# Global queries of a sparse attention: probabilities turned by transposes in two halves, their output on four column groups

## The reference, cut to what matters

```python
rel = k_idx[None, :] - q_idx[:, None]
local_ok = (rel <= 0) & (rel >= -(lw - 1))            # lw = 128
key_global = (k_idx % gs == 0)[None, :]               # gs = 64
query_is_global = (q_idx % gs == 0)[:, None]
allowed = (local_ok | key_global | query_is_global) & (rel <= 0)
scores = jnp.where(allowed[None, None], scores, -1e9)
w = jax.nn.softmax(scores, axis=-1)
out = jnp.einsum('bhtk,bhkd->bhtd', w, v)
```

## Time and profile before

| what | us |
|---|---|
| median of 3 runs | 3175.98 (3173.67 to 3176.52) |
| the profiled execution | 3170.18 |
| its span, from first to last record | 3168.2 |
| sparse attention in it, first matmul to last copy to `o_sb` | 1932.3 to 2534.9 |

### The profile page before, as it was taken

One profiled execution on the slowest core, in us unless ns is written; L12 is line 12 of the kernel. 1 busy time (PEld: TensorE's weight loads), 2 busy tenths in 40 slices (PEclk: granted clock), 3 DMA queues, 4 the chain that ended last, 5 costly groups with the idle time before them and its releaser, 6 DMA issues. The chain is left out here.

```text
span 3168.2 us, 105574 instructions
## 1 busy us (share of the span) xinstructions
PE 2955.8 (93%) x41356; PEld 2157.6 (68%) x41388; DVE 2607.4 (82%) x5505; ACT 1687.3 (53%) x3301; POOL 1076.7 (34%) x1434
## 2 busy tenths in 40 slices
PE   7989999999999799999997993999999969999999
PEld 4545777777777377777774552777777747777776
DVE  5759999999999499999985994777777669999997
ACT  4654888778887433333333661665665623333333
POOL 3551211212211122222223662555555612222222
PEclk9998999999999899999998996999999979999999
DMA  6664444444443222222223666455555322222221
GB/s 205 219 204 88 94 103 101 102 99 94 94 103 74 73 85 87 83 88 86 84 68 107 202 199 157 119 138 138 139 140 139 99 84 88 83 88 86 83 88 51
DMA packets 362150, 353.35 MB, mean 112 GB/s; under 512 B 79066, under 2 KB 298714, under 8 KB 361642
## 3 DMA queue, kind: packets, MB, share of 16 engines
q1 hardware_dynamic: 356003, 345.15, 39.6%
q10 hardware_dynamic: 5767, 2.68, 0.4%
HBM read 210.85 MB, written 135.27 MB: 109 GB/s over the span
## 5 line engine op out<-in xcount | busy, mean ns | idle before, releaser
L891 DVE TENSOR_REDUCE aA_nmax<-bank 128x1 f32<-128x512 f32 (+3 forms) x1216 | 715.0, 655 | 62.9 <-PE bank L952 56.8
L934 ACT ACTIVATE aA_prob<-bank 128x512 f32<-128x512 f32 (+1 forms) x1216 | 616.3, 581 | 196.2 <-PE bank L952 191.4
L952 PE MATMUL bank<-aA_ks,aA_qs 96*32 96x512 bf16 (+15 forms) x6144 | 512.5, 320 | 16.6 <-DMA aA_ks<-parts_A 12.7
L952 PE MATMUL bank<-aA_qs,aA_ks 99*32 99x512 bf16 (+11 forms) x6144 | 471.4, 314 | 7.0 <-ACT aA_prob L934 3.6
L875 POOL TENSOR_SCALAR_AFFINE_SELECT aA_prob<-aA_prob 128x512 f32<-128x512 f32 x256 | 160.9, 634 | 662.7 <-ACT aA_prob L934 662.7
L952 PE MATMUL bank<-aA_prob,aA_vq 128*32 128x512 f32 (+3 forms) x3072 | 356.1, 489 | 0.9 <-POOL aA_prob L875 0.9
L952 PEld LDWEIGHTS bank<-aA_ks,aA_qs 96*32 96x32 bf16 x6144 | 246.4, 96 | 125.6 <-DVE aA_nmax L891 45.2
L1382 ACT ACTIVATE aB_prob<-bank 128x512 f32<-128x512 f32 (+1 forms) x512 | 262.2, 574 | 88.1 <-PE bank L1421 84.4
L952 PEld LDWEIGHTS bank<-aA_qs,aA_ks 99*32 99x32 bf16 x6144 | 225.3, 96 | 62.6 <-ACT aA_prob L934 20.3
L1288 DVE TENSOR_REDUCE aB_nnear<-bank 128x3 f32<-128x480 f32 (+1 forms) x352 | 208.1, 636 | 57.0 <-PE bank L1421 52.1
L952 PE MATMUL bank<-mask_sb,ident_b 128*32 128x128 bf16 (+3 forms) x4096 | 237.8, 203 | 0.6 <-issue 0.5
(11 more groups left out here) (235 smaller groups left out, 6597.7 us busy)
## 6 DMA issues: line engine op xcount, KB each, us to landing
parts_A<-pA_part SPq DMA_DIRECT2D x96, 256.0 KB, 4.6
aA_qs<-parts_A SPq DMA_DIRECT2D x192, 128.0 KB, 4.0
parts_B<-pB_part SPq DMA_DIRECT2D x96, 256.0 KB, 2.6
aB_qs<-parts_B SPq DMA_DIRECT2D x192, 128.0 KB, 3.2
aA_ks<-parts_A SPq DMA_DIRECT2D x186, 128.0 KB, 4.0
aB_ks<-parts_B SPq DMA_DIRECT2D x186, 128.0 KB, 3.3
o_A<-aA_o_sb SPq DMA_DIRECT2D x32, 512.0 KB, 3.0
o_B<-aB_o_sb SPq DMA_DIRECT2D x32, 512.0 KB, 2.9
```

What stands on the lines that cost most here:

```text
L891: nc.vector.tensor_reduce(dst, src, AX.X, ALU.max, negate=True).then_inc(s["m_taken"], 1)
L934: nc.scalar.activation(dst, src, ACT.Exp, scale=SCALE).then_inc(s["e_taken"], 1)
L952: return nc.tensor.matmul(out, lhsT, rhs, start=start, stop=True, skip_group_check=True)
```

## The change

`gturn` becomes two units of four `nc.tensor.transpose` each (128 x 128, the whole identity as the moving side), one for each half of `pg`, each with its own bank of line "e" and its own copy. The copies read every second column of the bank. `og` becomes 32 narrow matmuls, for each block k of 128 keys and each head one with that head's 32 columns of `vq` as the weights and up to 16 columns of `pgT` as the moving side; the output of head h lies on partitions 32h to 32h + 31, in columns 0 to 15, and one copy takes all. In the table of tasks `gturn` has cost 500 twice (1150 before), ACT's part 400 twice (620), due -0.6 (-0.55); `og` has cost 1000 (1150), DVE's part 170 (500), due -0.4 (-0.35).

```diff
@@ sparse_tasks
         for c in range(2):
-            unit("e", "gexp", c, 180, "act", 710, -0.7, ("dve", "gmax", n, 1), then=[("act", "gturn", pre, 0)])
-        unit("e", "gturn", 0, 1150, "act", 620, -0.55, ("act", "gexp", n, 1), then=[("pe", "og", pre, 0)])
-        unit("m", "og", 0, 1150, "dve", 500, -0.35, ("act", "gturn", n, 0), ("pool", "vq", n, 0),
+            unit("e", "gexp", c, 180, "act", 710, -0.7, ("dve", "gmax", n, 1), then=[("act", "gturn", pre, c)])
+        for c in range(2):
+            unit("e", "gturn", c, 500, "act", 400, -0.6, ("act", "gexp", n, c), then=[("pe", "og", pre, 0)])
+        unit("m", "og", 0, 1000, "dve", 170, -0.4, ("act", "gturn", n, 1), ("pool", "vq", n, 0),
              then=[("dve", "lay", n - 2, 0)])
@@ take_og (DVE)
-                    src = bank_of("m", "og", n, 0)[:, 0:HQ * NGLOB].rearrange("p (h i) -> p h i", h=HQ)
-                    for h in range(HQ):
-                        mine = slice(2 * DH * h, 2 * DH * (h + 1))
-                        ins = nc.vector.tensor_copy(og[n % 2][mine, :], src[mine, h, :])
-                    ins.then_inc(s["m_taken"], 1)
+                    nc.vector.tensor_copy(og[n % 2][:, :], bank_of("m", "og", n, 0)[:, 0:NGLOB]).then_inc(s["m_taken"], 1)
@@ global_copy (ACT)
-                def global_copy(n, _):
-                    act.wait_ge(s["e_made"], after("e", "gturn", n, 0))
+                def global_copy(n, c):
+
+                    act.wait_ge(s["e_made"], after("e", "gturn", n, c))
                     if n >= 1:
                         act.wait_ge(s["m_made"], after("m", "og", n - 1, 0))
-                    nc.scalar.activation(pgT[:, :, :, :].rearrange("p k h i -> p (k h i)"), bank_of("e", "gturn", n, 0),
-                                         ACT.Copy).then_inc(s["e_taken"], 1)
+                    nc.scalar.activation(pgT[:, 4 * c:4 * c + 4, :, :].rearrange("p k h i -> p (k h i)"),
+                                         bank_of("e", "gturn", n, c)[:, ::2], ACT.Copy).then_inc(s["e_taken"], 1)
@@ global_turn, global_out (PE)
-                def global_turn(n, _):
-                    pe.wait_ge(s["e_taken"], max(after("e", "gexp", n, 1), bank_clear("e", "gturn", n, 0)))
-                    out = bank_of("e", "gturn", n, 0).rearrange("p (k i) -> p k i", k=QT)
-                    for k in range(QT):
-                        ins = mul(out[:, k, :], pg[:, k * P:(k + 1) * P], ident[:, ::2], True)
+                def global_turn(n, c):
+                    pe.wait_ge(s["e_taken"], max(after("e", "gexp", n, c), bank_clear("e", "gturn", n, c)))
+                    out = bank_of("e", "gturn", n, c).rearrange("p (k i) -> p k i", k=4)
+                    for k in range(4):
+                        ins = nc.tensor.transpose(out[:, k, :], pg[:, (4 * c + k) * P:(4 * c + k + 1) * P], ident[:, :])
                     ins.then_inc(s["e_made"], 1)
                 def global_out(n, _):
                     pe.wait_ge(s["vq_made"], n + 1)
-                    pe.wait_ge(s["e_taken"], after("e", "gturn", n, 0))
+                    pe.wait_ge(s["e_taken"], after("e", "gturn", n, 1))
                     need(pe, s["m_taken"], bank_clear("m", "og", n, 0))
-                    out = bank_of("m", "og", n, 0)[:, 0:HQ * NGLOB].rearrange("p (h i) -> p h i", h=HQ)
+                    out = bank_of("m", "og", n, 0)
                     for k in range(QT):
 
                         i0 = k * NGLOB // QT
-                        ins = mul(out[:, :, i0:], vq[n % 2][:, k, :, :].rearrange("p h d -> p (h d)"),
-                                  pgT[:, k, :, i0:], k == 0)
+                        for h in range(HQ):
+                            ins = mul(out[32 * h:32 * h + 32, i0:NGLOB], vq[n % 2][:, k, h, :], pgT[:, k, h, i0:], k == 0)
                     ins.then_inc(s["m_made"], 1)
```

## The result

The changed kernel takes 3197.86 us (median of 4 runs, 3196.51 to 3198.37), the kernel before 3174.82 in the same session: a ratio of 1.0073 (95% interval 1.0055 to 1.0090). It is slower by 23 us, where 50 us less had been forecast.

The account below looks back on a forecast made before the run. PE was taken to set the pace in sparse attention; savings of 0.50 (turn) and 1.35 us (output) per group, less 0.25 for waits, gave 32 x 1.60 = 51 us, a median of 3125 us, range 3101 to 3157.

Parts of the forecast that it names:

- What bounds the kernel: Sparse attention: PE sets the pace, with records for 484 of 500 us; DVE and ACT wait for it.
- The turn: Transposes of `pg` on PE: one pass each, 0.85 us per half, saving 0.50 us per group.
- The output on PE: `og` as 64 narrow passes at 11 ns: 0.70 us instead of 2.05, saving 1.35 us per group.
- The rival of a floor of 25 ns per pass: Narrow output passes cost 25 ns each, so the block takes 1.6 us; 3150 in all; chance 0.20.
- I take off 0.25 us per group for that: Sum: allowance for DVE and ACT bursts stopping PE more often, cutting 1.85 us saved per group to 1.60.
- POOL and SP get no work, and no DMA is added or moved: Other engines: the change adds no work for POOL or SP and no DMA, so nothing was counted.
- The slower rival: Halves of the turn stop PE, at 1.25 us each losing 0.65 us per group; 3197; chance 0.07.

Follow-up runs that it names:

- the control without loads: The kernel before, without the loads of q and k after the fourth group: 3170.82 us, ratio 0.9991 to the kernel before.

## Why the prediction was wrong

- **What bounds the kernel**: half right. PE sets the pace of the stage, but it has two limits, its work and its supply of instructions. Before, the supply was sufficient, with little to spare: the control without loads gains nothing and there are only 7 long stops, but packets were used up in as little as 3.1 us, where the next is usable after some 4.1.
- **The turn**: right. One pass per transpose, 0.77 us for a half (0.85 forecast).
- **The output on PE**: right, 0.79 us in the block shown and 0.54 to 0.67 in 17 of 32 groups (0.70). The rival of a floor of 25 ns per pass is refuted: 0.78 / 62 = 12.6 ns in the block shown, 9 to 11 in those 17 groups, with neighbouring passes in different column groups. The Trainium skill, TensorEngine Tiling, section Performance Considerations (Instruction Overhead), gives about 60 cycles per matmul, as an estimate 25 ns at 2.4 GHz; this trace doesn't agree.
- **"I take off 0.25 us per group for that"** is the step that failed. The new "issue" waits were 2.7 us per group, eleven times as much, and neither for line "e" nor for DVE. I had 42.1 us of "issue" in the earlier trace rows, called it a wait with no record that explains it, and didn't ask what it was. The count of records per packet was there to be read before, and so were the 7 long stops.
- **"POOL and SP get no work, and no DMA is added or moved"**: true of data, but 80 more PE instructions per group are DMA traffic too. I had counted passes, at 64 for 16, only as PE time. What I sold as a saving at both blocks, 4 us of 18 in which PE used few instructions, was what kept the supply ahead: no packet was used up in under 3.0 us then, and 26 in about 2.2 us now.
- **The slower rival** gave 3197 and the kernel took 3197.86, but by luck, for a reason that isn't so. It set the stops at the halves of the turn. The waits for the copy to `pgT` there are 4.9 us in 500, halves back to back don't help the narrow output, and the turn alone is faster.
- **The clock** was in no part of the forecast. It fell behind long stops and added some 0.6 us per group, by the estimate above.

## What to carry to other kernels

Count PE instructions, not only PE time, and look at the densest stretch, not at the mean: a packet of 252 must last until the next is there, here about 4 us. Splitting 8 wide matmuls into 32 narrow ones for 1.3 us of work paid in no run with its loads; without them the whole change paid 25 us, but what the split alone pays there wasn't run. "Issue" waits in mid-unit, a packet's worth of records apart, are the sign to look for, and here the loads of data made them worse. Where both limits are close, take the savings that also take instructions away, as the transposes did (16 fewer per group, and with a fitting order 24 us).

## What the runs showed of the hardware

- Instructions reach PE in packets of 16 KB, about 252 matmul and load records each. A packet is under way for 0.96 us; the 40 long stops of the changed kernel end 2.2 to 2.6 us after one has started.
- The next packet starts in the median 1.8 us after PE has begun on the one before, so PE stands where 252 records take less than some 4.1 us (an estimate from the medians). Packets of 2.2 us were followed by a long stop 25 times in 26.
- The same 80 instructions cost 14 us where slow blocks lie between, and 55 us where none do.
- With the DMA share at 0.17 instead of 0.53 the next packet starts 0.5 us sooner, and neither its transfer nor the time from its start to the end of the stop gets shorter (1.01 and 2.45 us, against 0.96 and 2.35). Whether it is bytes, descriptors or their bursts that hold the start up wasn't tried.
- Narrow f32 passes with 2 to 16 columns start 9 to 13 ns apart over four column groups, with weight loads of 128 x 32.
- An f32 transpose of 128 x 128 is one pass, where a matmul with the identity is two. The pitch is 0.110 us in the eights of projection B and 0.38 / 3 = 0.13 in the fours here, against 0.108 for the passes of the other kind.
